# Experts' outputs added to totals in DRAM by accumulating scatters, with the second half of the tokens routed between the blocks of the first

## The reference

```
x = x + _L0_attn_ref(_layernorm(x), ...)      # time mixing
x = x + _L0_xattn_ref(_layernorm(x), ctx, ...)
x = x + _L0_ffn_ref(_layernorm(x), ...)
x = x + _L1_attn_ref(_layernorm(x), ...)
x = x + _L1_xattn_ref(_layernorm(x), ctx, ctx)
x = x + _L1_ffn_ref(_layernorm(x), Wr, Wg, Wu, Wd)

def _L1_ffn_ref(x, Wr, Wg, Wu, Wd):           # E = 8 experts, K = 2
    probs = softmax(x @ Wr)
    topk_w, topk_idx = top_k(probs, K)
    topk_w = topk_w / sum(topk_w)
    for i in range(E):
        w_i = sum(topk_w * (topk_idx == i))
        h = silu(x @ Wg[i]) * (x @ Wu[i])
        output = output + w_i * (h @ Wd[i])
    return output
```

## Time and profile before

| | |
|---|---|
| median of 3 runs | 3057.93 us (3052.8 to 3058.66) |
| the profiled execution | 3063.06 us, its span 3060.9 us, granted clock 0.89 |
| busy share of the span | PE 80%, PEld 50%, DVE 70%, ACT 36%, POOL 34% |
| the last stage | from 2552 us to 3061 us of the span |
| first half routed, its scatters | 2552 to 2606, 2606 to 2649 |
| second half routed, its scatters | to 2675, 2680 to 2721 |
| blocks | from 2675, but most of them from 2725 to 3011 |
| sums after the last block | 3013 to 3056 |

### The profile page before, as it was taken

One profiled execution on the slowest core, in us unless ns is written; L12 is line 12 of the kernel. 1 busy time (PEld: TensorE's weight loads), 2 busy tenths in 40 slices (PEclk: granted clock), 3 DMA queues, 4 the chain that ended last, 5 costly groups with the idle time before them and its releaser, 6 DMA issues. The chain is left out here.

```text
span 3060.9 us, 69490 instructions
## 1 busy us (share of the span) xinstructions
PE 2449.2 (80%) x22172; PEld 1532.3 (50%) x22172; DVE 2149.1 (70%) x6125; ACT 1103.0 (36%) x2488; POOL 1045.4 (34%) x1535
## 2 busy tenths in 40 slices
PE   2555447999999974999888887599999997568882
PEld 1333324555555534999766665244444445434441
DVE  4999986787777866666589997577788874223343
ACT  1222213555555542222233332355566652012220
POOL 3444442222222214666544443222222220440124
PEclk8676768999999986999999998699999996579996
DMA  6000014443444410000000000533333330122333
GB/s 229 1 0 0 0 43 89 91 90 84 86 83 88 90 26 1 0 0 0 1 1 0 0 0 0 163 94 97 94 91 90 95 85 2 62 90 69 100 111 114
DMA packets 260951, 180.24 MB, mean 59 GB/s; under 512 B 36032, under 2 KB 255072, under 8 KB 259840
## 3 DMA queue, kind: packets, MB, share of 16 engines
q1 hardware_dynamic: 249920, 157.93, 20.3%
q0 software_dynamic: 6784, 17.02, 1.8%
q10 hardware_dynamic: 4160, 4.19, 0.5%
HBM read 94.10 MB, written 83.36 MB: 58 GB/s over the span
## 5 line engine op out<-in xcount | busy, mean ns | idle before, releaser
L736 ACT ACTIVATE xattn_pr<-ps 128x384 f32<-128x384 f32 (+1 forms) x1024 | 537.0, 544 | 489.1 <-PE ps L506 232.8
L610 DVE TENSOR_REDUCE xattn_mx<-ps 128x2 f32<-128x512 f32 x512 | 342.2, 679 | 127.8 <-PE ps L472 120.9
L485 PE MATMUL ps<-xattn_qp,xattn_kp 128*128 128x192 bf16 (+1 forms) x2048 | 416.0, 264 | 2.1 <-DMA xattn_qp<-xattn_mrow 1.8
L472 PE MATMUL ps<-xattn_kp,xattn_qp 96*128 96x192 bf16 (+1 forms) x2048 | 372.6, 264 | 34.4 <-DMA xattn_kp<-xattn_rows 29.2
L606 DVE CUSTOM_DVE_ANT_0 xattn_masked<-ps,xattn_band 128x192 bf16<-128x192 f32 x1024 | 323.7, 353 | 100.4 <-issue 45.1
L485 PEld LDWEIGHTS ps<-xattn_qp,xattn_kp 128*128 128x128 bf16 x2048 | 164.0, 98 | 282.3 <-ACT xattn_pr L736 152.5
L506 PE MATMUL ps<-xattn_pr,xattn_vs 128*32 128x256 f32 (+1 forms) x4096 | 303.4, 368 | 0.0
L506 PE MATMUL ps<-xattn_pr,xattn_ones 128*32 128x256 f32 (+1 forms) x4096 | 303.2, 368 | 0.0
L472 PEld LDWEIGHTS ps<-xattn_kp,xattn_qp 96*128 96x128 bf16 x2048 | 189.0, 99 | 68.7 <-issue 22.1
L2415 POOL TENSOR_TENSOR attn_kmask<-attn_k,const_sb 128x1024 f32<-128x1024 f32 x64 | 154.0, 2425 | 189.9 <-ACT attn_k L2292 189.9
L488 PE MATMUL ps<-xattn_band,xattn_ident 128*128 128x192 bf16 x1024 | 211.7, 247 | 0.0
(11 more groups left out here) (306 smaller groups left out, 4797.2 us busy)
## 6 DMA issues: line engine op xcount, KB each, us to landing
xattn_rows<-xattn_parts SPq DMA_DIRECT2D x128, 192.0 KB, 2.0
xattn_qp<-xattn_rows SPq DMA_DIRECT2D x256, 96.0 KB, 2.8
xattn_kp<-xattn_rows SPq DMA_DIRECT2D x256, 96.0 KB, 3.2
xattn_rows<-xattn_parts SPq DMA_DIRECT2D x128, 128.0 KB, 1.9
moe_xb<-moe_rows_in SPq DMA_DIRECT2D x78, 128.0 KB
moe_rows_out<-moe_yb SPq DMA_DIRECT2D x78, 128.0 KB
moe_rows_in<-region_zero SPq DMA_DIRECT2D x8, 1024.0 KB, 10.6
xattn_rows<-xattn_parts SPq DMA_DIRECT2D x128, 64.0 KB, 1.7
```

What stands on the lines that cost most here:

```text
L472: mm = nc.tensor.matmul(ps[:, BANK_S + j % RING, mt * D:mt * D + width], qp[u][s][0:R_MAX, h, mt * P:(mt + 1) * P], kp[u][s][0:R_MAX, h, l ...
L485: mm = nc.tensor.matmul(out, kp[u][s][:, h, nt * P:(nt + 1) * P], qp[u][s][:, h, lo:lo + width], start=True, stop=not banded)
L610: ins = nc.vector.tensor_reduce(mx[s][:, h * NT:(h + 1) * NT], ps[:, BANK_S + j % RING, :].rearrange("p (m n) -> p m n", m=NT), AX.X, ALU.max)
L736: nc.scalar.activation(out, src, ACT.Exp, scale=HD ** -0.5).then_inc(exped, 1)
```

## The change

Routing of the second half is cut into pieces that stand between the blocks of the first half on PE, ACT and DVE (the tables `NORMED` to `MOVED`): a pair per block, a group's steps spread over five blocks, the count behind block 22 and the table in DVE's turn 23. POOL starts the second half's 32 scatters from block 24 on, 4 after each block's output, over 8 blocks.

The rows that are scattered get two more numbers: the token's row and its weight for this expert. So a row is 258 numbers (`ROW`), each pair is kept in two copies (`row[0]`, `row[1]`), and ACT makes the second (`copy_row`). At the stage's start SP writes x to `moe_total` in DRAM, and for each block DVE multiplies the output with its weights while it copies it out (`keep_y`), and POOL adds the 128 rows to `moe_total` with one indirect DMA that accumulates (`add`). Each such DMA waits until the one before it has landed. Gathers, sums and the stores of each pair and each block are gone; instead `moe_total` is copied to the output, the first half after the load of block 45, the second at the end. The load of block n waits for the accumulation of block n - 6.

PE's order in a turn n becomes turn hidden of n, turn rows of n + 3, gate and up of n + 2, down of n. `clear_regions` fills longer rows with fewer, larger DMAs, and gives unused rows spare row numbers.

```diff
+    NORMED = {i: [PP + i] for i in range(PP)}
+    TURNED = {i + 1: [PP + i] for i in range(PP)}
+    LOGITS = {i + 2: [PP + i] for i in range(PP)}
+    FULL = {(k + 1) * G + 1: PER + k for k in range(PER)}
+    EXPS = {n + 1: g for n, g in FULL.items()}
+    RANKS = {n + 2: g for n, g in FULL.items()}
+    PLACES = {n + 3: g for n, g in FULL.items()}
+    CHOICES = {n + 4: g for n, g in FULL.items()}
+    COUNT = max(CHOICES) + 1
+    MOVED = COUNT + 2
...
-                    wait(sp, xb_turned, n - RB + 1)
+                    wait(sp, added, 16 * (n - RB + 1))
...
                 for n in range(N):
-                    if n + 2 < N:
-                        e[n + 2] = expert_of(n + 2)
-                    if n + 1 < N:
-                        gate_up(*divmod(n + 1, BLOCKS), e[n + 1])
-                    turn_hidden(*divmod(n, BLOCKS))
-                    if n + 2 < N:
-                        turn_block(*divmod(n + 2, BLOCKS))
-                    down_product(*divmod(n, BLOCKS), e[n])
+                    turn_hidden(n)
+                    if n + 3 < N:
+                        turn_block(n + 3)
+                    if n + 2 < N:
+                        e[n + 2] = gate_up(n + 2)
+                    down_product(n, e.pop(n))
+                    for p in LOGITS.get(n, []):
+                        logit_product(p)
+                    for p in TURNED.get(n, []):
+                        turn_x(p)
+                    if n in PLACES:
+                        places(PLACES[n])
+                    if n == COUNT:
+                        count(1)
...
-                    wait(v, yb_left[n % RB], 16 * uses(n, n % RB, RB))
-                    nc.vector.tensor_copy(yb[n % RB][:], ps[:, BANK_D, 0:D]).then_inc(y_kept, 1)
+                    wait(v, added, 16 * (n - 3))
+                    nc.vector.tensor_scalar(yb[n % 4][:], ps[:, BANK_D, 0:D], xb[n % RB][:, D + 1:D + 2], None, ALU.mult).then_inc(y_kept, 1)
...
+                def add(n):
+                    part, b = of(n)
+                    g.wait_ge(xb_in[n % RB], 16 * (n // RB + 1))
+                    wait(g, added, 16 * (n - RB + 1))
+                    nc.gpsimd.tensor_copy(to[n % RB][:], xb[n % RB][:, D:D + 1]).then_inc(to_made, 1)
+                    if b == 0:
+                        g.wait_ge(begun[part], 16)
+                    g.wait_ge(to_made, n + 1)
+                    g.wait_ge(y_kept, n + 1)
+                    wait(g, added, 16 * n)
+                    g.indirect_dma_start(total[part], bass.IndirectOffsetOnAxis(ap=to[n % RB][:, 0:1], axis=0), yb[n % 4][:], None,
+                                         compute_op=ALU.add).then_inc(added, 16)
...
+                for n in range(N):
+                    add(n)
+                    if n == MOVED:
+                        g.wait_ge(tabled, 2 * TABLE)
+                    if MOVED <= n < MOVED + PP // 2:
+                        for p in range(PP + 2 * (n - MOVED), PP + 2 * (n - MOVED) + 2):
+                            scatter(p)
```

More of the change, by code:

```diff
@@ L1384, in sem @@
             return core.sem(f"{name}_{n}")
-        xn = sb("xn", [P, PAIRS, D])
+        row = [sb(f"row{k}", [P, PAIRS, ROW]) for k in range(2)]
         xt = [sb(f"xt{u}", [P, NT, P]) for u in range(2)]
@@ L1419, in routed_experts, with of, bank_free @@
         xb_in = [sem(f"xb_in{r}") for r in range(RB)]
-        xb_turned, xb_kept, gu_made, tanhed, hidden = (sem(n) for n in ("xb_turned", "xb_kept", "gate_up", "tanh", "hidden"))
+        gu_made, tanhed, hidden = (sem(n) for n in ("gate_up", "tanh", "hidden"))
         h_turned, h_kept, downed, y_kept = (sem(n) for n in ("h_turned", "h_kept", "down", "y_kept"))
-        yb_left = [sem(f"yb_left{r}") for r in range(RB)]
-        y_in = [[sem(f"y{k}_in{r}") for r in range(RY)] for k in range(2)]
-        summed = sem("summed")
-        left = [sem(f"out_left{u}") for u in range(2)]
-        def idx(part, b):
-            return part * BLOCKS + b
-        def uses(n, r, ring):
-            return (n - r + ring - 1) // ring
-        def blocks():
-            return [(part, b) for part in range(PARTS_R) for b in range(BLOCKS)]
-        def sums_after(part, b):
-            if part == 0:
-                return []
-            return range(PP * b // BLOCKS, PP * (b + 1) // BLOCKS)
+        begun = [sem(f"total_begun{h}") for h in range(PARTS_R)]
+        to_made, added, left = sem("to_made"), sem("added"), sem("out_left")
+        def of(n):
+            return divmod(n, BLOCKS)
+        order = [("pair", p) for p in range(PP)] + [("block", n) for n in range(3)]
+        for n in range(N):
+            if n + 3 < N:
+                order.append(("block", n + 3))
+            order += [("pair", p) for p in TURNED.get(n, [])]
+        turn = {what: k for k, what in enumerate(order)}
+        kept_before = {}
+        for k, (what, i) in enumerate(order):
+            kept_before[k] = (sum(w == "pair" for w, _ in order[:k]), sum(w == "block" for w, _ in order[:k]))
+        def bank_free(pe, k):
+            if k >= 2:
+                pairs, blocks = kept_before[k - 1]
+                if order[k - 2][0] == "pair":
+                    pe.wait_ge(x_kept, pairs)
+                else:
+                    pe.wait_ge(xb_kept, blocks)
         with nc.Block() as block:
@@ L1470, in _, with store_out @@
-                for p in range(PAIRS - PP, PAIRS):
-                    store_out(p)
-                for u in range(2):
-                    sp.wait_ge(left[u], 16 * (PAIRS // 2))
+                def store_out(part):
+                    sp.wait_ge(added, 16 * BLOCKS * (part + 1))
+                    rows = out_dram.rearrange("n t d -> (n t) d")
+                    for q in range(4):
+                        each = REGION // 4
+                        sp.dma_start(rows[part * REGION + q * each:part * REGION + (q + 1) * each, :].rearrange("(a b) d -> a (b d)", b=4),
+                                     total[part][q * each:(q + 1) * each, :].rearrange("(a b) d -> a (b d)", b=4)).then_inc(left, 16)
@@ L1475, in _ @@
+                for part in range(PARTS_R):
+                    sp.dma_start(total[part][0:REGION, :].rearrange("(n q) d -> q n d", q=P),
+                                 core.x[:, part * PP:(part + 1) * PP, :]).then_inc(begun[part], 16)
+                for n in range(N):
+                    load_block(n)
+                    if n == BLOCKS + RB:
+                        store_out(0)
+                store_out(1)
+                sp.wait_ge(left, 16 * 4 * PARTS_R)
             @block.tensor
@@ L1782, in _ @@
-                make_hidden(0, 0)
-                for n, (part, b) in enumerate(blocks()):
-                    if n + 1 < N:
-                        make_hidden(*divmod(n + 1, BLOCKS))
-                    keep_y(part, b)
-                    for p in sums_after(part, b):
-                        add_up(p)
-                for p in range(PAIRS - PP, PAIRS):
-                    add_up(p)
+                block_table(0)
+                make_hidden(0)
+                for n in range(N):
+                    if n + 1 < N:
+                        make_hidden(n + 1)
+                    if n > 0:
+                        keep_y(n - 1)
+                    for p in NORMED.get(n, []):
+                        normalise_x(p)
+                    if n in EXPS:
+                        less_maximum(EXPS[n])
+                    if n in RANKS:
+                        ranks(RANKS[n])
+                    if n in CHOICES:
+                        choices(CHOICES[n])
+                    if n == COUNT + 1:
+                        block_table(1)
@@ L1792, in _ @@
+                keep_y(N - 1)
             @block.gpsimd
```

237 lines of the change are left out of this document (106 added, 131 removed).

## The result

The changed kernel takes 3068.29 us (median of 7 runs, 3067.37 to 3070.04), the kernel before 3056.92 us (7 runs, 3052.8 to 3058.66). The ratio is 1.0042, with a 95% interval of 1.003 to 1.0053: slower by 11 us, where 48 us less than 3057.93 had been forecast. The time lies inside the stated range, whose upper part takes in the slow rival, but not where the forecast had it, and the sign is the other one. The profiled execution has a span of 3066.5 us; the forecast for it was 3012.7.

The account below looks back on a forecast made before the run. A chain of routing, scatters, PE's blocks and gathers was taken to set the end. Turn 0 at 2662.9 plus turns, routing, scatters, copy, end, accumulation and stalls gave span 3012.7, median 3010 us; 8-in-10 range 2970 to 3095.

Parts of the forecast that it names:

- the slow rival: Blocks: the chain of accumulating DMAs bounds every turn at 2.41 + e; slower from e = 2.1, turn 4.55; chance 0.2.
- Kernel start, +2.7: Kernel start: longer POOL fill, a copy and wait, and SP's eight larger DMAs cost 2.7 us more (0 to 4).
- First scatters 42.4 us: Start of last stage: 32 scatter issues at 1.27 us and the last landing, 42.4 us to a block's first load, kept.
- A turn is 3.42: Block loop on PE: the idle 0.40 us goes, 3.82 to 3.42 us a turn, 266.8 us for 78 turns.
- e is 1.1: Accumulating DMA: e, its time beyond a plain scatter's 2.41 us, is 1.1; chain wants 3.51 us a turn, +5 us.
- Scatters between blocks +24: POOL between blocks: four scatters and an accumulation take 6.4 us a turn for 8 turns, against 3.42: +24 us.
- copy +6: SP's queue ahead of block 46's load: copying the first half's totals, 5.3 us, with four issues +6 us.
- Stalls by the scatters +6: Blocks beside the second half's scatters: time lost to stalls, +6 us (0 to 30).
- routing +18.4: Second half's routing between blocks: PE's pairs 9.4 us and count 9.1 us at 2.4 GHz, +18.4 us.
- DVE +8: Second half's routing between blocks: `keep_y` comes late behind DVE's rank steps, table and choices, +8 us (0 to 14).
- The rival in which scatters starve ACT and DVE: Eight scatter turns: ACT and DVE are starved again, +30 us instead of +6, 3034 us; chance 0.17.
- End 15.4: Kernel end: `keep_y`, the last accumulation, four issues and copying 2.1 MB to the output take 15.4 us.

Follow-up runs that it names:

- the kernel with the new order: The kernel before with only the order of the blocks' steps taken from after, and six row buffers in place of four: 2998.51 us, ratio 0.9813.
- The plain-scatter run: After, with each block's accumulating scatter made plain (no adding, the wait for the one before kept): 3007.11 us, ratio 0.9838.

## Why the prediction was wrong

The forecast for the span was 3012.7, the trace has 3066.5, 53.8 more. Step by step:

- **Kernel start, +2.7.** It was -2.5. SP's eight issues took 8.2 us in place of 10.79, the lower bound's kind, and the longer fill (2.89 us) did not outweigh that. The +2.7 also stands above what the step's own terms allow: with the 1.45 they give -0.7 to +2.3.
- **Start of the last stage.** Nothing was counted for the stages between; they cost 14.5 us (12.0 late in spite of 2.5 gained). This is the address shift, a cause that no step or rival had. It puts turn 0 at 2670.45, forecast 2662.9. The 14.5 is rather low, since the profiled execution of before was 6 us above its median: the kernel with the new order, the same up to here, starts its last stage at 2546.2, not 2552.5.
- **First scatters 42.4 us, routing of the first half +0.8.** Right: scatters from 2618.84 to a first load at 2660.78 are 41.9, and the stage's start to the first scatter took 0.5 us more than before.
- **"A turn is 3.42".** PE could do 3.02. The mechanism was right, the gain was sized too small: 0.80 and not 0.40, of which 0.56 at the wait and 0.24 in the groups behind it. It did not matter, since PE did not bind.
- **"e is 1.1", the step that failed.** By the forecast's own measure, link = 2.41 + e, e was 4.52 - 2.41 = 2.11, its upper bound. The plain-scatter run takes this apart: 0.79 of it has nothing to do with adding. The 2.41 was read where SP waits for POOL's scatter and moves at once; a chain in which POOL waits for its own DMA needs 0.78 us more from landing to the next issue, while the landing itself comes after 2.42 us, as there. Adding itself costs 1.32, near the 1.1. The step that was mis-sized is the link of a plain chain, 2.41 where 3.20 was measured, and by the sum's own formula that alone turns 3.51 into 4.3.
- **Scatters between blocks +24, copy +6.** The copy took 5.3, as forecast. The eight scatter turns took 7.17 us and not 6.4, since an accumulation holds POOL longer than a scatter and a cast stands before it; that they still add only 21 us is because they are counted above a link of 4.52 and not above 3.42. The sum agrees by luck.
- **Stalls by the scatters +6, routing +18.4, DVE +8.** Hidden in the chain, but for one turn of 6.28 us in which POOL waits 4.24 us for DVE's output behind the table (1.8 above a link). The rival in which scatters starve ACT and DVE did not come: in the eight turns POOL's own issues fill the time, with 0.3 us between them.
- **End 15.4.** 13.8 from the last accumulation's issue at 3052.7 to 3066.5; forecast 14.8 from the same point. (A slip of the sum: 3001.5 and 5 are 3006.5, not 3006.7.)

From turn 0 to the last accumulation the forecast had 335 us (2662.9 to 2997.9), the trace 382. That is 47 of the 54; turn 0's 7.5 is the rest but for 1 us in the end. The slow rival named this mechanism and its deciding point, a turn of 4.55. The turn was 4.52, and with the address shift taken out the time was even with before, as this break-even says. So the 0.2 for that rival was low: I chose the middle between the ends of e, 0 and 2.1, and read the link's other part at an engine that doesn't take part in the chain. That e came out at the upper bound, 2.1, is luck, as that bound was built from other parts.

The Trainium skill, Collectives: The Full Stack (The bandwidth ceiling: the fold count and why AG ≠ RS ≠ AR), puts a reducing transfer's slowness down to a second source read and not to the adding. The e of 0.3 that the forecast took from it was too little: the transfer alone took 0.74 longer.

What stays open: why POOL's issue of an accumulation takes 0.58 us more, what the 0.78 us between landing and next issue consist of, and why among addresses off 256 those off 64 too are slower.

## What to carry to other kernels

If each transfer of a chain waits for the landing of the one before, price a link at the engine that waits and issues, from issue to next issue, and not at another that was released by such a transfer. Two targets that alternate, or a slot for each writer, take the chain away; then the ring of input buffers is next and wants more depth. A change can hold a large gain (here 57 us for an order) that another of its parts hides, so try each alone. And when stages slow down that no line of the diff touches, compare the DMA engines' busy share there at equal bytes, and look at whether a table that grew has moved the tiles behind it.

## What the runs showed of the hardware

- An accumulating indirect DMA of 128 rows of 1 KB to DRAM takes 3.5 to 3.9 us from issue to landing, mostly near 3.75, a plain one 2.42; chained on POOL, 4.52 and 3.20 us. With two in flight, to different tensors, they went at PE's pace of 3.01 us, and single ones as close as 2.04.
- Moving the DMA targets of a stage from a multiple of 256 bytes by an odd multiple of 32 costs some 13 us (the second wide attention, 623 to 629 us at a multiple of 256 bytes, 636 to 642 at odd multiples of 32), with all engines' busy times unchanged; 29 unused columns of constants cost the whole kernel 23 us.
- Groups of four matmuls on PE that follow without a stop stand 0.86 and 1.72 us apart from start to start; in turns with a 0.40 us wait ahead of the down product the same two took 1.00 and 1.82.
